# Four lanes of a gated cross-attention network: the turns of the lanes written out in a new order

## What is computed

```python
x = x + jnp.tanh(g_xattn[0]) * _L0_xattn_ref(_layernorm(x), ctx_768, ...)   # 16 heads of 16
x = x + jnp.tanh(g_ffn[0])   * _L0_ffn_ref(_layernorm(x), ...)    # ternary weights, conv, silu
x = x + jnp.tanh(g_xattn[1]) * _L1_xattn_ref(_layernorm(x), ctx_768, ...)   # 16 heads of 64
x = x + jnp.tanh(g_ffn[1])   * _L1_ffn_ref(_layernorm(x), ...)    # one of 8 experts for each token
x = x + jnp.tanh(g_xattn[2]) * _L2_xattn_ref(_layernorm(x), ctx_768, ...)   # 16 heads of 16
x = x + jnp.tanh(g_ffn[2])   * _L2_ffn_ref(_layernorm(x), ...)    # self-attention, then an MLP
x = x + jnp.tanh(g_xattn[3]) * _L3_xattn_ref(_layernorm(x), ctx_768, ctx_768, ...)
x = x + jnp.tanh(g_ffn[3])   * _L3_ffn_ref(_layernorm(x), ...)    # 3 blocks of two linear maps
```

## Time and profile before

| | |
|---|---|
| runs: lowest, median, highest | 2829.98, 2832.99, 2834.33 us |
| the profiled execution: span from first to last instruction | 2829.7 us |
| the profiled execution's own time | not stated apart from its span; the median of the runs is 3.3 us above the span |
| busy: PE, PEld, DVE, ACT, POOL | 2597.7, 2122.2, 2187.3, 1684.6, 1134.9 us |
| mean granted TensorE clock | 0.975 |

### The profile page before, as it was taken

The page is one execution under the profiler, slowest core; times in us unless marked ns, Lnnn a source line. Parts: engine busy times, 40 slices in busy tenths (PEclk is TensorE's granted clock), DMA queues, the critical chain, the costliest instruction groups (busy, mean ns, idle before and its releaser), DMA issues.

```text
span 2829.7 us, 60900 instructions
## 1 busy us (share of the span) xinstructions
PE 2597.7 (92%) x23748; PEld 2122.2 (75%) x23748; DVE 2187.3 (77%) x4794; ACT 1684.6 (60%) x4539; POOL 1134.9 (40%) x1981
## 2 busy tenths in 40 slices
PE   7797989899888989999899999999999999999999
PEld 5676767677666767777777777888787878788777
DVE  7868697877678587786767777787878787778998
ACT  4565666666555666666555555655656565656544
POOL 2132323323443543324454444333333333435676
PEclk9898999999899999999999999999999999999999
DMA  6000000000011121100012121100000000000110
GB/s 189 3 24 9 18 13 18 14 13 18 11 48 40 63 77 42 30 16 24 11 46 62 55 76 58 33 19 20 21 16 21 16 24 13 24 3 25 33 36 21
DMA packets 84168, 92.15 MB, mean 33 GB/s; under 512 B 15332, under 2 KB 77288, under 8 KB 83880
## 3 DMA queue, kind: packets, MB, share of 16 engines
q1 hardware_dynamic: 75432, 59.91, 6.9%
q0 software_dynamic: 8448, 28.34, 3.4%
HBM read 65.36 MB, written 22.85 MB: 31 GB/s over the span
## 4 chain that ended last, share of the span: by engine, by line
PE 63%; DVE 23%; ACT 5%; POOL 4%; issue 3%; DMA 1%; SPq 1%; DVEq 0%; POOLq 0%; ACTq 0%
PE psum L353 14%; PE psum L377 12%; PE psum L346 12%; PE psum L403 6%; DVE tiny L730 4%; PE psum L415 3%; PE psum L532 3%; DVE big L738 3%; PE psum L370 3%; PE psum L360 3%; PE psum L367 2%; PE psum L526 2%; PE psum L513 2%; DVE xn L711 1%; DVE tiny L766 1%
## 5 line engine op out<-in xcount | busy, mean ns | idle before, releaser
L377 PE MATMUL psum<-ident,big 128*128 128x128 f32 x2784 | 428.2, 285 | 66.2 <-ACT big L1219 22.4
L377 PEld LDWEIGHTS psum<-ident,big 128*128 128x128 f32 x2784 | 324.0, 145 | 140.2 <-ACT big L1219 49.3
L1219 ACT ACTIVATE big<-big 128x512 f32<-128x512 f32 x512 | 312.1, 631 | 170.4 <-DVE big L738 168.5
L730 DVE TENSOR_REDUCE tiny<-psum 128x8 f32<-128x1024 f32 x256 | 312.3, 1220 | 47.5 <-PE psum L403 42.8
L738 DVE TENSOR_TENSOR big<-psum,tiny 128x512 f32<-128x512 f32 x512 | 329.6, 685 | 8.8
L1382 POOL TENSOR_SCALAR tiny<-mv 128x1 f32<-128x1 f32 x224 | 53.0, 236 | 677.1 <-DVE mv L701 674.9
L403 PE MATMUL psum<-head_keys,small 64*128 64x256 f32 x2048 | 285.9, 403 | 19.7 <-ACT big L1226 10.9
L1399 POOL TENSOR_TENSOR head_keys<-big,head_rows 128x512 f32<-128x512 f32 x256 | 266.6, 1060 | 0.0
L1424 POOL TENSOR_TENSOR big<-big,tiny 128x512 f32<-128x512 f32 x128 | 133.8, 1052 | 308.2 <-DVE tiny L773 308.0
L403 PEld LDWEIGHTS psum<-head_keys,small 64*128 64x128 f32 x2048 | 185.3, 189 | 74.6 <-issue 56.9
L1263 ACT ACTIVATE big<-psum,tiny 128x128 f32<-128x128 f32 x512 | 181.7, 382 | 38.1 <-DVE tiny L768 37.6
(11 more groups left out here) (334 smaller groups left out, 6616.7 us busy)
## 6 DMA issues: line engine op xcount, KB each, us to landing
ctxT<-in_ctxT SPq DMA_DIRECT2D x64, 128.0 KB, 2.2
after_L_xattn<-x SPq DMA_DIRECT2D x64, 128.0 KB, 1.7
mixture_out<-spare SPq DMA_DIRECT2D x46, 128.0 KB, 1.7
x_in<-in_x SPq DMA_DIRECT2D x32, 128.0 KB, 2.2
mixture_in<-xn SPq DMA_DIRECT2D x32, 128.0 KB, 1.7
x_in<-after_L_xattn SPq DMA_DIRECT2D x32, 128.0 KB, 2.1
w_bits<-after_L_xattn SPq DMA_DIRECT2D x32, 128.0 KB, 2.1
spare<-in_L_w SPq DMA_DIRECT2D x2, 1024.0 KB, 7.2
```

The lines of the kernel that those rows point to most:

```text
L377: last = pe.transpose(bank[:, k * P:(k + 1) * P], src[:, k * P:(k + 1) * P], identity)
L730: dve.tensor_reduce(top, s8, AX.X, ALU.max).then_inc(*t.dve.tell(p, f"{l}.top{r}"))
L1219: last = act.activation(flat, flat, ACT.Exp, scale=DH ** -0.5)
```

## The change

Only the strings of `ORDER` are replaced. No piece is added, dropped or altered: each engine's string has the same length and the same count of each lane as before, and within a lane the pieces follow in the same order. Characters that differ at their place: PE 2136 of 3144, DVE 1473 of 2291, ACT 2002 of 3022, POOL 780 of 1244, SP 231 of 341. The new order puts turns of the same array tile shape next to each other and places what feeds TensorE first.

```diff
 ORDER = {
     "pe": (
-        "3231314231212111323213121121213234230231023113100222200033331111313121323210301301030101131030200123"
...
+        "1113132321324211313231221312312313242332021111320330222310111000110030302130203213213130111032103213"
...
     "dve": (
-        "1302130424413214213411441213221321323022131131313133132131212232321321301322203103030000100130120020"
...
+        "1013223143421432144314412031312321321121311212131310122130332323230231321302010203213301211230200003"
...
     "act": (
-        "3323211312121111332232132111122212333233002103110122002002133133332211111133100030130103313110032202"
...
+        "1111333223211123123311132221313223321322321011101332012203230010231031002100001133131321302132113032"
...
 }
```

More of the change, by code:

```diff
@@ new lines @@
+        "1231320202113011320203203030221321023230230101232022301331313000013321330021012112100313202302301101"
+        "2313223121002010321231231330332021132021302311310321020313122321013103122302003002230232223303031203"
+        "2130122133010101300031121020112110210203230203010303213123200100221213231323013301231203211210231102"
+        "3010312131200202113013102200230323320120331032102132031031321322320103013031301021210120020120323020"
+        "3013212123122213231213300030231232121331031022102302312321312103130101213211301322103020023302302102"
@@ new lines @@
+        "3231322223103010301311030210130320332012100102120021230201301010302301200302131321323121020123103103"
+        "1202103012012101332312123120121120120130131123103022023032232021302310203212301023212123310310313033"
+        "0032320131232001032313030210101201032030231100032202122123213231030132102101331231023131021323023120"
+        "1201231231230130220211301310002023212310232030103232231023031031031303000131332310021021200101203102"
+        "0231312000023121322013120230120131301022031131203233112312012101030202302303121123321310220202302323"
@@ new lines @@
+        "3230331231023111322302103023010002030013211331301223202312031303231030101123112102111023212223201030"
+        "2300301032133878273083873270827a9a938a7a987093708a9707380a803abc9c97b8a79800aba78bc00898c0b78a9ac7ba"
+        "8bc8799cab980a87c8b9ab79c88ab7a8c0b9a8b78ab79abcc890cbaa7076a75c695bc65b6c59ab6957c6ac567959c89b7a65"
+        "8b956c6859bcb6565ab65cc9a6c56bc59ca6957b86c56ab75c9a6b5c87b56a57ca6798a859856c65cb67979679a65b5c6c8b"
+        "5c69a865b95a76bcb5876ca69b585b6c76a5b679875a6b5698cba76ca5895c668b57957c56b9acb56786595cb65"
@@ L277 @@
-        "8bcac7a076599b565bc6ca5657968cb658ca7b695"
+        "3101113332222032001121113220332000111320232133002001132122333200013110120223331103220013011022131213"
+        "20230313000222301031112223313103000002321112123233002011023603217138023230511010a122132b2241433c0330"
+        "2090301022112113420303304210402121340332001123212443000431123220331004421124433001723878ab798bc8aa98"
+        "ab07c79ac655669558c96bc7b65ab9ca78596bc65"
     ),
```

180 lines of the change are left out of this document (81 added, 99 removed).

## The result

The changed kernel takes 2759.08 us (median of 4 runs, 2756.83 to 2766.47) against 2833.66 us beside it: ratio 0.9739, 95% interval 0.9726 to 0.9753. The profiled execution is the longest of the four, so its span of 2765.2 us shows 64.5 us of the gain.

A forecast was written before the change was run, and what follows sets the result against it. TensorE was taken to bound the kernel, with 232 us idle to win from. Terms -7 - 8 - 4 + 3 = -16 us on the 2829.7 us span, plus 3.3, gave 2817 us; range 2780 to 2858.

The forecast's parts named there:

- Shape changes: TensorE's order: 75 fewer changes of array shape between turns, at 0.094 us each, save 7.0 us.
- the other reading: Shape changes on TensorE: if each drain left the last matmul's whole 0.27 us unshared, some -12 us.
- The waits before `pT`: TensorE's L377 waiting for VectorE's L832, 19.5 us in 11 waits: more turns now stand before pT, saving 8 us.
- What is nearer now: First transpositions of a stage (L377 waiting for L711): some distances to the normalised input get shorter, costing 3 us.
- The clock: TensorE at half clock in three stretches of 13.7, 10.2 and 13.6 us: -4 us, at best -13.
- Hidden: ScalarE's table loads, 12 before and 10 after, and moved SP and POOL turns: 0 us.
- Rival B: Feeding TensorE first works everywhere, a fifth of its 232 us idleness goes: 2780 us; chance 0.20.
- Rival D: Slower: ScalarE holds ready turns back behind turns that are not ready; +35 us, 2852 us; chance 0.25.
- C: First half bound by VectorE's queue, so saved shape changes become waits and pT's wait moves: 2833 us; chance 0.13.
- E: Longer runs of transpositions on TensorE lower its clock: +37 us, 2854 us; chance 0.02.
- signs that I gave for "right": Lower TensorE idleness and L832 wait, shorter half-clock stretches, higher mean clock, and both halves' work done earlier.
- A: The likeliest case, all terms as summed: about -16 us, 2817 us; chance 0.40.

The follow-up runs named there:

- pt_repair: Kernel before, with nine pT turns (and rows2) 1 to 6 turns later and ten second tanh turns of ScalarE 1 or 2 earlier: 2882.80 us, ratio 1.0151.
- the two halves: Changed order only up to pass 7's route turns, the old one after: 2788.21 us (0.9826); the reverse: 2821.59 us (0.9945).
- held_low: Changed order, turns moved on all engines for early inputs and fewer VectorE steps held by GpSimd, 1,095 shape changes: 2806.40 us, ratio 0.9881.
- waits_only: Kernel before, turns moved a few places on all engines for earlier TensorE inputs, shape changes kept at 1168: 2875.49 us, ratio 1.0131.

## Why the prediction was wrong

The time by its own terms, for the profiled executions (-64.5 us). As the span is busy time and idle time of TensorE, -39.2 of it is idleness and -25.3 busy time; how the busy time splits is an estimate.

- **Shape changes, -7.0: the price held.** At full clock (of each kind of step the quickest fifth ends there) the next matmul starts 109 ns after a transposition pass with the same shape and 202 after one when the shape changes; for L371 216 and 313, L513 111 and 208, L403 216 and 313. That is 93 to 97 ns in four kinds of turn, in both kernels. 75 changes fewer at this price are 7 us. A drain that costs a whole unshared matmul of 0.27 us (the -12 us of the other reading) is excluded by these.
- **The waits before `pT`, -8: right in kind, too small.** The wait fell by 14.0 us, to 5.5. But `pt_repair` shows that it can't be counted alone: there it fell by 15.0 and the kernel was 44 us slower. It was also not the second largest cause of TensorE's idleness, as the prediction read it, but the fourth: L1219 (22.4 us) and L1424 (20.0) stood between the two rows.
- **What is nearer now, +3: wrong in sign.** L377 for L711 fell from 22.8 to 14.0 us. The distances in TensorE's own work got shorter and the waits too. L711 itself ran shorter (513 ns in the mean for 588), held less often by GpSimd; whether the rest is a norm that began earlier, I didn't separate.
- **The step that failed: the sum took two kinds of wait (L832 and L711) for the whole.** They were 42 of 232 us of idleness, and the sum gave -8 + 3 = -5 us for them. The rest was set at nothing without a row to say so. Measured, idleness went down by 39.2 us: 22.8 in those two rows and 16.4 in the rest. In the rest the waits for ScalarE, 99.2 us in 170, lost 24.3 and those for GpSimd 3.7, while VectorE's other waits grew by 9.9 (idle pieces under 0.15 us are in no such row). The idle term is 34 of the 48 us that the forecast lacks.
- **The clock, -4 with -13 as the bound: far too small.** I took three half-clock stretches of 37.5 us out of 144.7, and 58.3 us of half clock went. Within the half-clock time TensorE was busy for 107.9 us before and for 71.7 after. Half of these 36.2 us is 18. Together with the 7 of the shape changes that is 25, and TensorE's busy time fell by 25.3. So -7 - 18 - 39 = -64, against -64.5 measured. The prediction also tied the three stretches to the wrong wait: it says that they came after the waits for `pT`, but all three began before those ended, two of them some 5 us before the wait for `pT` had even begun (399.6 against 404.5 us, 706.8 against 711.6). They shrank without going.
- **Hidden, 0:** nothing speaks against it; transfers are 1% of the chain.

Rival B (a fifth of the idleness, everywhere) had the size of the idle term about right: it put 46 us, and 39 went. Its 2780 us lacks the clock; with the 18 us measured for it, it would have been 2762. Whether B's reason is the true one, that what feeds TensorE comes first, no run shows. Rival D counted ScalarE turns behind ones whose input comes later, 498 before and 804 after, and called it a loss. ScalarE's waits after and before:

```profile
ACT big L1219 <- DVE big L738: 205.3, 163, 4.2
...
ACT xnT L1193 <- PE psum L377: 64.1, 60, 4.1
...
ACT big L1174 <- PE psum L371: 48.4, 44, 8.2
ACT small L1174 <- PE psum L346: 46.8, 47, 6.2
```

```profile
ACT big L1219 <- DVE big L738: 168.5, 134, 6.3
ACT big L1174 <- PE psum L371: 100.5, 63, 8.2
...
ACT small L1174 <- PE psum L346: 49.6, 56, 3.6
...
ACT xnT L1193 <- PE psum L377: 44.4, 37, 3.5
```

D's sign was more waiting for TensorE before L1174, L1193 and L1226. Over the three lines it fell from 258.5 to 217.2 us, but not everywhere: the kind of wait by which D was argued (L1174 for L346) stayed about the same, L1193's grew, and the fall is in L1174 for L371. More is waited for VectorE, and TensorE's waits for ScalarE shrank all the same. The count took TensorE's own work as the clock and VectorE as free at once, so it couldn't tell. C fell with the span; E fell too: half-clock time shrank with longer runs of transpositions.

Of the signs that I gave for "right", all came, most of them far beyond what was written: idleness 192.8 (about 220), L832 5.5 (under 12), the three stretches shorter, the clock 0.985 (over 0.975), 100 to 1500 us earlier by some 50 (10 or more), the rest by 19 (2 to 4). They could not tell A from B, since each had a bound on one side only.

What isn't shown is which feature of the new order makes the inputs come in time. No order of mine gave that gain; the two halves did, each in its own stretch. That feeding TensorE first is the cause was only argued.

## What to carry to other kernels

Where the bound engine idles in hundreds of waits under 3 us, price all of them by the engine that is waited for, and give the half-clock time a term of its own size: it brought about half as much again here (18 us on 39). The two don't keep step in general: `held_low` has 217 us of idleness and 89 at half clock, `waits_only` 257 and 136, the kernel before 232 and 145. Compare a stretch of low clock with the same work in the other trace, not with the same time. Look too whether it began before or after the wait that it is put down to. Here no move of single turns and no order with one engine's string taken over gave a part of the gain, so a new order of all queues is better cut in time, as the two halves were. When a small edit costs more than its mechanism, run a copy that moves nothing before blaming the move.

## What was not expected of the hardware

- **VectorE is held by GpSimd for whole steps.** In the traces of the two given kernels 127 steps of L711 began while a GpSimd tensor step (L1399, L1424, L1411, L1419, L1555) ran that lasted longer than the L711 step takes alone. 121 of them ended 130 to 170 ns after the GpSimd step, and none before it. So did all 39 such steps of L817 and L821. Other steps weren't held: of L738, which reads PSUM, 41 of 44 ended before the GpSimd step, and of the statistics L699 51 of 52. This agrees with the Trainium skill, SBUF — State Buffer, Who interferes with whom, by which a VectorE step in a two-port mode and a GpSimd step exclude each other for the whole of the instruction, and one with two SBUF inputs contends with a GpSimd step that reads SBUF. In all, the steps over 0.15 us longer than their like cost VectorE 97 us before and 90 after.
- **A done-signal of TensorE can come up to 7.5 us after the recorded end** of its matmuls (4.9 in the wait shown above). Most such waits lie near the two groups of L1498's transfers. Waits with no releaser found are in the traces of all the kernels made here and in neither of the given ones, run twice each.
- **64 tiny fp32 matmuls in the setup aren't hidden:** they ran from 3.2 to 30.7 us and put off the first turn by 21 us (32 of them, to 17.0, by 7), and nothing later made up for it.
